# Main weights of the first tile cast into ten places and written back by SyncE, in an eight-core transformer layer

## The reference

```
n   = layernorm(x)
xp  = silu(n @ W_in.T)
a   = sigmoid(xp @ W_alpha.T + b_alpha);  b = sigmoid(xp @ W_beta.T + b_beta);  v = tanh(xp @ W_v.T + b_v)
h_t = a_t * h_(t-1) + b_t * v_t                 (a scan over the 4096 tokens)
x   = x + (h * silu(h)) @ W_out.T
n   = layernorm(x);  r = rmsnorm(n)
q   = r @ Wq + bq;  k, v = split(((r @ Wdown + bdown) @ Wup + bup) as 16 heads of 2*64)
att = softmax over the 16 heads of one token (16 x 16 per token), o = att @ v
u   = n + o @ Wo + bo
m   = rmsnorm(u);  gate = softmax(m @ Wg + bg) over 8 experts
out = x + u + sum over e of gate_e * (m @ We_e)
```

## Time and profile before

| what | us |
|---|---|
| median of 3 runs (lowest, highest) | 2054.05 (2053.99, 2067.32) |
| the profiled execution, its own time | 2057.98 |
| its span on the slowest core (core 4) | 2056.3 |
| spans of the 8 cores | 2047.8 to 2056.3 |
| granted clock of the 8 cores, share of full | 0.973 to 0.975 |

### The profile page before, as it was taken

The page is one execution under the profiler, slowest core; times in us unless marked ns, Lnnn a source line. Parts: engine busy times, 40 slices in busy tenths (PEclk is TensorE's granted clock), DMA queues, the critical chain, the costliest instruction groups (busy, mean ns, idle before and its releaser), DMA issues.

```text
span 2056.3 us, 32761 instructions; the slowest of 8 cores (2047.8 to 2056.3 us)
## 1 busy us (share of the span) xinstructions
PE 1931.7 (94%) x11239; PEld 909.0 (44%) x11456; DVE 1259.1 (61%) x2106; ACT 721.7 (35%) x1905; POOL 220.2 (11%) x222
## 2 busy tenths in 40 slices
PE   5756799999999999999999999999999999999899
PEld 2323444444444454444444444444544444444444
DVE  2457546765577646776468655776467764676544
ACT  2236442423443323542334334433235424342100
POOL 4543000110002000020001100020000200011000
PEclk9986799999999999999999999999999999999999
DMA  9999996775433364334543354333643344423344
GB/s 277 308 331 162 181 177 165 173 176 188 181 123 124 126 223 146 121 124 154 195 144 124 124 199 170 123 124 130 218 150 118 124 155 154 142 103 124 123 143 164
DMA packets 49456, 334.77 MB, mean 163 GB/s; under 512 B 5952, under 2 KB 6080, under 8 KB 14464
## 3 DMA queue, kind: packets, MB, share of 16 engines
q1 hardware_dynamic: 42112, 271.43, 38.1%
q0 software_dynamic: 7184, 61.23, 13.6%
HBM read 318.37 MB, written 48.23 MB: 178 GB/s over the span
## 4 chain that ended last, share of the span: by engine, by line
PE 86%; DMA 7%; issue 2%; DVE 2%; POOL 1%; ACT 1%; DVEq 0%; SPq 0%; ACTq 0%; POOLq 0%
PE bank L352 40%; PE bank L407 14%; PE bank L453 6%; PE bank L421 5%; PE bank L533 5%; PE bank L392 5%; DMA we<-wscr 3%; DMA wscr<-wm 2%; PE bank L482 2%; PE bank L508 2%; PE bank L469 2%; PE bank L518 2%; PE bank L505 1%; DMA we<-wall 1%; PE bank L434 1%
## 5 line engine op out<-in xcount | busy, mean ns | idle before, releaser
L352 PE MATMUL bank<-we,h2T 128*128 128x512 bf16 x3966 | 922.3, 380 | 22.1 <-DVE gat L888 6.6
L700 DVE SCALAR_TENSOR_TENSOR xs<-bank,gat,xs 128x512 f32<-128x512 f32 x512 | 383.9, 750 | 443.6 <-PE bank L352 443.4
L352 PEld LDWEIGHTS bank<-we,h2T 128*128 128x128 bf16 x4096 | 387.2, 98 | 443.2 <-issue 30.0
L407 PE MATMUL bank<-F,wm 128*128 128x512 bf16 x1504 | 336.7, 383 | 15.4 <-POOL wm L274 12.9
L287 POOL TENSOR_TENSOR pb<-pb,sml 128x512 bf16<-128x512 bf16 x128 | 132.9, 1038 | 1437.6 <-DVE sml L815 1437.6
L655 ACT ACTIVATE pb<-bank,sml 128x128 bf16<-128x128 f32 x512 | 181.2, 367 | 217.9 <-DVE sml L807 208.1
L407 PEld LDWEIGHTS bank<-F,wm 128*128 128x128 bf16 x1536 | 151.2, 99 | 199.8 <-issue 22.8
L421 PE MATMUL bank<-wm,F 128*128 128x512 bf16 x497 | 113.1, 384 | 11.6 <-POOL wm L274 10.8
L453 PE MATMUL bank<-F,wm 128*128 128x512 bf16 x503 | 120.8, 380 | 0.4
L755 DVE SCALAR_TENSOR_TENSOR R<-R 128x512 f32<-128x512 f32 x64 | 48.3, 754 | 117.2 <-ACT R L610 117.2
L533 PE MATMUL bank<-wm,F 128*128 128x512 bf16 x496 | 112.4, 383 | 1.8 <-DVE F L844 1.1
(11 more groups left out here) (84 smaller groups left out, 1642.1 us busy)
## 6 DMA issues: line engine op xcount, KB each, us to landing
we<-wscr SPq DMA_DIRECT2D x128, 1024.0 KB, 4.8
wm<-wscr SPq DMA_DIRECT2D x98, 1024.0 KB, 5.8
wscr<-wall POOLq DMA_DIRECT2D x16, 1024.0 KB, 15.9
out<-xs SPq DMA_DIRECT2D x32, 512.0 KB, 4.5
wscr<-wm POOLq DMA_DIRECT2D x14, 1024.0 KB, 24.9
xs<-x SPq DMA_DIRECT2D x7, 2048.0 KB, 11.0
xs<-wall POOLq DMA_DIRECT2D x12, 1024.0 KB, 22.6
we<-wall POOLq DMA_DIRECT2D x10, 1024.0 KB, 22.0
```

The lines of the kernel that those rows point to most:

```text
L352: mm = pe.matmul(b[:, :], hT[:, kc * 512 + tb * 128:kc * 512 + (tb + 1) * 128], we[ui % NE][:, kc * 512:(kc + 1) * 512], start=(kc == 0), ...
L407: mm = pe.matmul(bk[(mc % 2) * 3 + j][:, :], w[:, (ci % 4) * 1024 + kc * 128:(ci % 4) * 1024 + (kc + 1) * 128], F2[:, kc * 512:(kc + 1) * ...
L700: v.scalar_tensor_tensor(dst, bk[6 + k % 2][:, :], gat[(t - 1) % 2][:, tb * 8 + e:tb * 8 + e + 1], dst, OP.mult, OP.add).then_inc(v_ec, 1)
```

## The change

The main units of tile 0 no longer go through three places but through ten: w0s lists the place of each of the 14 units (wm[0], wm[1], wm[2], tm1, h2T[0], the two halves of qt, the two halves of kt, and again wm[0], wm[1], wm[2], h2T[0], wm[0]). w0prev gives the unit whose write-back must land before a place is used again; the first nine units wait for none. GpSimd no longer issues the write-backs. SyncE does (wb): unit 0 after 12 casts, units 1 to 9 after 20, units 10 to 13 one by one after W_out and after load_x(1). The masks qm and km are loaded by SyncE after the write-backs of units 5 to 8 have landed; the two bias tensors bgb and bob are loaded at the start. ACT waits for the write-backs of units 5 and 6 ahead of its first write of q, DVE for those of 7 and 8 ahead of its first write of k, and for 12 ahead of its first write of h2T[0]. The points at which GpSimd issues the expert casts are set anew.

```diff
@@ -102,6 +102,9 @@
     gex = sb("gex", [128, 32], F32)
     gat = [sb(f"gat{i}", [128, 32], F32) for i in range(2)]
 
+    w0s = [wm[0], wm[1], wm[2], tm1, h2T[0], qt[:, 0:4096], qt[:, 4096:8192], kt[:, 0:4096], kt[:, 4096:8192],
+           wm[0], wm[1], wm[2], h2T[0], wm[0]]
+    w0prev = [None] * 9 + [0, 1, 2, 4, 9]
     stgh = [xs[2][:, 0:2048], xs[2][:, 2048:4096]] + [t[:, :].bitcast(F32) for t in (h2T[1], we[0], we[1])]
 
     vt = R3[:, :].bitcast(BF16)
@@ -160,7 +163,7 @@
                 return
             u = idx % NMU
             if idx < NMU + NM:
-                sync.wait_ge(s_cv[idx - NM], 16)
+                sync.wait_ge(s_cv[(11, 13, 10)[idx - NMU]], 16)
             if idx < 2 * NMU:
                 sync.wait_ge(s_cv[u], 16)
             sync.dma_start(out=wm[idx % NM][:, :],
@@ -186,6 +189,9 @@
             sync.dma_start(out=xs[sl][:, :].rearrange("p (b f) -> p b f", f=D),
                            in_=xin[t * TT:(t + 1) * TT, :].rearrange("(b p) f -> p b f", p=128)
                            ).then_inc(s_x[sl], 16)
+
+        def wb(u):
+            sync.dma_start(out=wscr[u * 128:(u + 1) * 128, :], in_=w0s[u][:, 0:4096]).then_inc(s_cv[u], 16)
 
         done = [0]
 
@@ -212,17 +218,21 @@
             m0 = t * NMU
             if 2 <= t + 1 < NT:
                 load_x(t + 1)
-            sync.wait_ge(p_win, t * 8 + 4)
-            load_m(m0 + 3)
-            sync.wait_ge(p_win, t * 8 + 8)
-            load_m(m0 + 4)
             if t == 0:
-                sync.dma_start(out=qt[64:72, :], in_=qm_d).then_inc(s_c2, 16)
-                sync.dma_start(out=kt[64:72, :], in_=km_d).then_inc(s_c2, 16)
                 sync.dma_start(out=bgb[:, :], in_=bgb_d).then_inc(s_c2, 16)
                 sync.dma_start(out=bob[:, :], in_=bo_d).then_inc(s_bo, 16)
+                sync.wait_ge(c_cm, 12)
+                wb(0)
+                sync.wait_ge(c_cm, 20)
+                for u in range(1, 10):
+                    wb(u)
+            else:
+                sync.wait_ge(p_win, t * 8 + 4)
+                load_m(m0 + 3)
+                sync.wait_ge(p_win, t * 8 + 8)
+                load_m(m0 + 4)
             ec(t, A_WIN)
-            for i in range(6):
+            for i in range(6 if t > 0 else 0):
                 sync.wait_ge(p_abv, t * 24 + 4 * i + 4)
                 load_m(m0 + 5 + i)
             ec(t, A_ABV)
@@ -231,7 +241,14 @@
             sync.wait_ge(p_wout, t * 8 + 8)
             load_m(m0 + 12)
             if t == 0:
+                for u in range(5, 9):
+                    sync.wait_ge(s_cv[u], 16)
+                sync.dma_start(out=qt[64:72, :], in_=qm_d).then_inc(s_c2, 16)
+                sync.dma_start(out=kt[64:72, :], in_=km_d).then_inc(s_c2, 16)
                 load_x(1)
+                for u in range(10, 14):
+                    sync.wait_ge(c_cm, 2 * u + 2)
+                    wb(u)
             ec(t, A_WOUT + A_T2)
             sync.wait_ge(p_wq, t * 8 + 4)
             load_m(m0 + 13)
@@ -241,7 +258,7 @@
                 for i in range(NE):
                     load_e(i)
             ec(t, A_S0 + A_ATT + A_WO)
-            sync.wait_ge(p_wo, t * 8 + 7)
+            sync.wait_ge(p_wo, t * 8 + (7 if t > 0 else 8))
             load_m(m0 + 15)
             sync.wait_ge(p_wo, t * 8 + 8)
             load_m(m0 + 16)
@@ -257,25 +274,24 @@
                          in_=wall_d[u * 128:(u + 1) * 128, hf * 2048:(hf + 1) * 2048]).then_inc(s_ld[h % 5], 16)
 
         def cm(u):
-            f = u - NM
-            if f >= 0:
+            f = w0prev[u]
+            if u == 3:
+                gp.wait_ge(p_t1, 4)
+            if f is not None:
                 if f < 2:
                     gp.wait_ge(p_win, 4 * f + 4)
                 elif f < 8:
                     gp.wait_ge(p_abv, 4 * (f - 1))
-                elif f < 10:
-                    gp.wait_ge(p_wout, f - 1)
                 else:
-                    gp.wait_ge(p_wq, 4)
+                    gp.wait_ge(p_wout, 8)
                 gp.wait_ge(s_cv[f], 16)
             for hf in range(2):
                 h = 2 * u + hf
                 gp.wait_ge(s_ld[h % 5], 16 * (h // 5 + 1))
-                gp.tensor_copy(wm[u % NM][:, hf * 2048:(hf + 1) * 2048], stgh[h % 5]).then_inc(c_cm, 1)
+                gp.tensor_copy(w0s[u][:, hf * 2048:(hf + 1) * 2048], stgh[h % 5]).then_inc(c_cm, 1)
                 gp.wait_ge(c_cm, h + 1)
                 if h + 5 < 2 * NMU:
                     ld(h + 5)
-            gp.dma_start(out=wscr[u * 128:(u + 1) * 128, :], in_=wm[u % NM][:, :]).then_inc(s_cv[u], 16)
 
         def ce(e):
             u = NMU + e
@@ -304,26 +320,30 @@
         ce(0)
         cm(13)
         ce(1)
+        gp.wait_ge(p_wdn, 1)
+        ce(2)
+        gp.wait_ge(p_wq, 6)
+        ce(3)
         for j in range(16):
             pnorm(0, j)
             if j % 4 == 1:
-                ce(2 + j // 4)
-        gp.wait_ge(p_wo, 8)
-        ce(6)
+                ce(4 + j // 4)
         gp.wait_ge(p_win, 8 + 2)
-        ce(7)
+        ce(8)
         gp.wait_ge(p_abv, 24 + 4)
-        ce(8)
-        gp.wait_ge(p_abv, 24 + 16)
         ce(9)
-        gp.wait_ge(p_wout, 8 + 2)
+        gp.wait_ge(p_abv, 24 + 14)
         ce(10)
+        gp.wait_ge(p_abv, 24 + 24)
+        ce(11)
+        gp.wait_ge(p_wout, 8 + 8)
+        ce(12)
         gp.wait_ge(p_wq, 8 + 4)
-        ce(11)
+        ce(13)
         for j in range(16):
             pnorm(1, j)
-            if j % 4 == 2:
-                ce(12 + j // 4)
+            if j in (2, 8):
+                ce(14 + j // 8)
         for t in range(2, NT):
             for j in range(16):
                 pnorm(t, j)
@@ -357,8 +377,8 @@
         def wait_m(idx):
             if idx < NMU:
                 pe.wait_ge(c_cm, 2 * idx + 2)
-            else:
-                pe.wait_ge(s_wm[idx % NM], 16 * len(range(idx, NMU - 1, -NM)))
+                return w0s[idx]
+            pe.wait_ge(s_wm[idx % NM], 16 * len(range(idx, NMU - 1, -NM)))
             return wm[idx % NM]
 
         def t1(t):
@@ -579,6 +599,8 @@
                 s.wait_ge(v_nm1, t + 1)
                 if t > 0:
                     s.wait_ge(p_t1, t * 4)
+                if t == 1:
+                    s.wait_ge(s_cv[3], 16)
             s.activation(out=tm1[:, b * D:(b + 1) * D], in_=xs[t % 3][:, b * D:(b + 1) * D],
                          func=AF.Identity, scale=sml[:, R1 + b:R1 + b + 1],
                          bias=sml[:, N1 + b:N1 + b + 1]).then_inc(a_l1a, 1)
@@ -633,6 +655,9 @@
                          bias=cph[:, 48:49]).then_inc(a_z, 1)
             for mc in range(NCH):
                 s.wait_ge(p_wq, t * 8 + mc + 1)
+                if t == 0 and mc == 0:
+                    s.wait_ge(s_cv[5], 16)
+                    s.wait_ge(s_cv[6], 16)
                 qv = qt[0:64, :].rearrange("p (g s) -> p g s", s=128)
                 for hl in range(2):
                     h = 2 * mc + hl
@@ -792,6 +817,9 @@
             for hd in range(16):
                 v.wait_ge(p_wup, t * 16 + hd + 1)
                 b = bk[(3, 4, 5, 2)[hd % 4]]
+                if t == 0 and hd == 0:
+                    v.wait_ge(s_cv[7], 16)
+                    v.wait_ge(s_cv[8], 16)
                 kv = kt[0:64, :].rearrange("p (g s) -> p g s", s=128)
                 v.tensor_scalar_add(kv[:, :, hd * 8:hd * 8 + 8],
                                     b[0:64, :].rearrange("p (g i) -> p g i", i=8),
@@ -860,6 +888,8 @@
                             OP.mult).then_inc(v_nb3, 1)
             ec(t, A_T3 - 2)
             for kc in range(NCH):
+                if t == 0 and kc == 0:
+                    v.wait_ge(s_cv[12], 16)
                 if kc % 2 == 0:
                     v.wait_ge(p_t3, t * 4 + kc // 2 + 1)
                 bb = bkb[(4, 5, 0, 1)[kc // 2]]
```

## The result

The changed kernel takes 2090.9 us against 2054.6 before. The ratio is 1.0165, with a 95% interval of 1.0139 to 1.0191: slower, by some 34 to 36 us, where +7 was forecast, and outside the range of 2036 to 2077. In one of its four executions, and in some of the other kernels, the cores of a die show a lower granted clock than the rest; the times given from here on are medians without those executions. The profiled execution took 2090.6 us.

What follows compares the result with a forecast made beforehand. The first 300 us were taken as one long DMA programme, with TensorE the bound after 360 us. Terms -20.3 (start of Wq) + 22.4 (kt held) + 0 + 5 gave +7 us, a median of 2061; range 2036 to 2077.

Steps and rivals of the forecast that it cites:

- The x tile: Load for tile 1, behind the masks on SyncE: wanted at some 175, costed at nothing, 5 us at most if late.
- the slow queue: SyncE's queue beside expert casts: 2.88 MB in 55 us, 19 us per MB, applied to write-backs and unit 0.
- Equal turns: Two DMA queues share packet for packet, so a write-back beside main-unit loads gets half the rate, 6.4 us each.
- The first term, the gates and W_out: Tile 0: gates end at 85.1, W_out starts at 93.6 with the 20th cast, Wq 20.3 us sooner.
- kt held for unit 8: Tile 0, ahead of DVE's first k write: unit 8's write-back lands at 151, scores start at 168.7; +22.4 us.
- ACT's wait for units 5 and 6: Tile 0: write-backs landed at 138, the wait covered by DVE's own wait.
- Main units of tile 1: 0: Second gate unit of tile 1 lands at 276.2, wanted at 276.5: no wait, 0; bounds 0 and +8.
- The cast behind W_out: +5: Tile 1: a cast beside the expert loads behind W_out, where TensorE ran dry, costs +5 us; bounds 0 and +9.
- The slower one: Rival: SyncE's queue falls behind, W_in of tile 1 waits 12 us, gate units some 8; 2081 us, chance 0.15.

Runs made afterwards that it cites:

- c: Changed kernel with SyncE's order kept and expert casts 1 to 7 all issued in the attention of tile 0, none ahead of it: 2073.6 us.
- a: Changed kernel with load_x(1) issued ahead of the waits for write-backs 5 to 8 and ahead of the masks: 2068.3 us.
- b: Changed kernel with load_x(1) still behind the waits for write-backs 5 to 8, but ahead of the two mask loads: 2072.3 us.
- f: Run a with expert cast 12 issued after Wdown of tile 1 instead of behind its last W_out group: 2057.3 us.
- k: Kernel before the change with expert cast 10 issued behind the last W_out group of tile 1 instead of the second: 2066.7 us.
- g: Run a with all of GpSimd's expert cast points as in the kernel before the change: 2052.7 us (two executions).
- i: The same kernel as g, run again for its time: 2056.5 us (twelve executions), ratio 1.0005 to the kernel before.

## Why the prediction was wrong

- **The x tile is the step that failed.** "The masks, behind unit 9, are wanted only at 168 and the x tile at some 175; both stand ahead of the casts that GpSimd issues from about 160 on, so I cost them at nothing; if they slip, DVE waits [...] 5 us at most." The wait was 31.1 us. The casts came at 153.9, not 160; unit 9 landed 53.1 us after its issue at 96.1, at 149; and the masks lay between. A margin of 6 us was left for a transfer that took 12 to 13.5 us in c, with no cast beside it. The bound of 5 us was not worked out: with what I had used in the next paragraph (2.88 MB in 55 us beside casts, rows 8) 2 MB come to 40 us, and x in packets half as large as theirs to more. I had applied the slow queue to the write-backs and not to x.
- **Equal turns** The earlier trace rows were read rightly, but only between loads of main units. For casts I used a mean rate. The rule that turns go by packet and not by bytes was in the same rows: 462 and 459 packets, 3.36 and 1.87 MB.
- **The first term, the gates and W_out.** The gates end at 87.2 (forecast 85.1), with no wait for a cast: right. W_out starts at 99.0, not 93.6, and what it waits for is DVE (11.8 us), not the 20th cast, which was there at 90. For why DVE was late, see the last section. The 5 us were without effect, since k was held anyway.
- **kt held for unit 8.** Forecast 151, DVE's wait some 20 us; measured 20.4 us, ended at 148, scores at 165.3 against 168.7 forecast. The size of the term holds: from the 20th cast to the landing the forecast had 57 us, 51 for eight write-backs at 6.4 us and 6 for a cast; unit 8 landed 52.2 us after its issue. Two errors cancel in this. The whole cast (issued at 127.2, landed 14.0 us later) was served ahead of unit 8, not two thirds of it, and the write-backs had more than half the rate in the end: from 140 to 148 us GpSimd's queue moved nothing and SyncE's 2.42 MB. ACT's wait for units 5 and 6 (12.3 us) ended ahead of DVE's, as forecast.
- **Main units of tile 1: 0.** 0.8 us on one core, nothing on the others, as forecast. In part this is luck: where tile 1 came 30 us late for x, its loads had time to spare. Cores 1 and 7, which never waited for x, had no such wait either, but with x out of the way it is up to 3 us on three cores of a and up to 9 us in b and c.
- **The cast behind W_out: +5.** Right in mechanism; it was 9.3 us on core 6, against 3.4 on core 4 before. The size was too small: by itself (f against a, k against before) it is worth about 11 us.
- **The rivals.** The slower one named the right queue and the right cause, write-backs and casts ahead of something wanted, but the wrong thing: W_in of tile 1 never waited. Its time of 2081 came nearer than the forecast.

## What to carry to other kernels

List for each DMA that is moved, not only for the large ones, when it is wanted and what runs beside it then, and price it in turns: the number of its packets for each DMA engine times the length of the other queue's packet. Where two queues meet, a transfer in small packets goes ahead of the large ones or waits until they are through. Where DMA engines are full over a stretch, a stall taken away at its start can come back at its end: in g and i the waits for casts in the gates and ahead of W_out are gone, DVE waits 15 to 24 us for kt instead, and the time is that of the kernel before. Whether fewer bytes would win there was not tested.

## What the runs showed of the hardware

The expert casts' packets are large: 4.19 MB in 176 packets, 24 KB each, 93% of 16 engines for 40 us. As an estimate from that row, one holds an engine for 3.4 us (0.93 x 16 x 40 / 176). One of these beside each 4 KB packet slows a queue to 0.74 MB in 40 us, 18 GB/s, where q1 moved 1.87 MB in 16 us beside q0's packets of 7.3 KB.

The race is a matter of few us. On cores 1 and 7 x was issued at 142.7 and 143.7 and DVE never waited for it; on core 3 at 144.8, 7.3 us of waiting; on cores 0, 2 and 6 at 147.6 to 148.4, 30 to 31 us. Core 4 (146.0, 29.5 us) and core 5 (146.3, 8.8 us) show that the moment of issue is not all of it. What counts is how much of x is through by 158 us, when the packets of the casts have come. In the DMA view from 140 to 158 us the packets under 8 KB, less those under 2 KB, are those of x. Core 4, then core 5:

```profile
DMA packets 693, 4.19 MB, mean 233 GB/s; under 512 B 50, under 2 KB 50, under 8 KB 442
```

```profile
DMA packets 845, 5.03 MB, mean 280 GB/s; under 512 B 63, under 2 KB 63, under 8 KB 526
```

On core 4, 392 of 512 were through, on core 5 463, on core 6 361; on core 3 all but 4, and those still cost 7.3 us. On core 6, 44 of x's 54 us went to the last 30% of it. Why x moved faster on core 5 before the casts came is not known.

DVE is slower while GpSimd casts. In the gates of tile 0, where the casts now follow one another without waits, the four DVE lines of the gates took 41.9 us for 32 instructions from 43 to 108 us, against 32.0 before. The same instruction of DVE, beside a cast of GpSimd and away from one, and the casts of that time (changed kernel, core 6):

```profile
67.32 2.32 DVE L773 TENSOR_TENSOR F<-R 128x512 bf16<-128x512 f32 x1
...
73.64 0.67 DVE L773 TENSOR_TENSOR F<-R 128x512 bf16<-128x512 f32 x1
```

```profile
66.52 2.58 POOL L291 CAST kt<-we 128x2048 bf16<-128x2048 f32 x1 [0.28 <-DMA we<-wall]
...
74.58 1.90 POOL L291 CAST kt<-xs 128x2048 bf16<-128x2048 f32 x1 [4.40 <-DMA xs<-wall]
```

The slow one starts while the cast runs and ends just behind it. From the last gate matmul to W_out it is 11.8 us, where the forecast had 5.2. A slower DVE would account for the difference, and so for W_out's start at 99.0; this is argued, since no run took GpSimd's casts away to test it.
